# Twelve of 49 node tiles summed by fetched rows instead of eleven, fourteen fetches to nine steps, and their products in the bank of the transposes

## The reference

```python
h = jnp.maximum(_layernorm(x, axis=-1), 0.0)
x = x + _L0_gnn_ref(h, edge_index, edge_attr_64, W1, b1, W2, b2)   # mean of edge features, then a 2-layer MLP
h = jnp.maximum(_layernorm(x, axis=-1), 0.0)
x = x + _L1_gnn_ref(h, src, dst, w_neigh, w_self, b_self)

# _L1_gnn_ref(feat, ...):
summed = jax.ops.segment_sum(feat[src], dst, num_segments=n)
deg = jax.ops.segment_sum(jnp.ones_like(dst, dtype=feat.dtype), dst, num_segments=n)
h_neigh = (summed / jnp.maximum(deg, 1.0)[:, None]) @ w_neigh.T
rst = feat @ w_self.T + b_self + h_neigh
```

## Time and profile before

| | us |
|---|---|
| median of 3 runs | 1132.64 (1132.23 to 1134.74) |
| the profiled execution | 1135.44 |
| its span, first to last instruction | 1133.5 |
| first layer and edge lists | 0 to 455 |
| last preparation, PE nearly idle | 455 to 467.4 |
| loop over 38 dense tiles, with 11 near tiles between | 467.4 to 1130 |
| PE busy / DVE / ACT / POOL in the span | 1072.6 / 787.8 / 494.5 / 521.7 |
| mean granted clock | 0.985 |

### The profile page before, as it was taken

One profiled execution on the slowest core, in us unless ns is written; L12 is line 12 of the kernel. 1 busy time (PEld: TensorE's weight loads), 2 busy tenths in 40 slices (PEclk: granted clock), 3 DMA queues, 4 the chain that ended last, 5 costly groups with the idle time before them and its releaser, 6 DMA issues.

```text
span 1133.5 us, 29643 instructions
## 1 busy us (share of the span) xinstructions
PE 1072.6 (95%) x11380; PEld 792.0 (70%) x11380; DVE 787.8 (70%) x1849; ACT 494.5 (44%) x957; POOL 521.7 (46%) x502
## 2 busy tenths in 40 slices
PE   3689999999999999699999999999999999999998
PEld 2667777777777777467767777677677777776765
DVE  6778878887883667766766676766676767666762
ACT  4455646342212546444444444444444444444441
POOL 3011111110002664377576766774767676677520
PEclk9899999999999999699999999999999999999999
DMA  8776655555562221133233233332333333333210
GB/s 259 226 212 202 198 162 166 153 162 161 173 198 93 77 61 44 51 98 104 79 108 96 86 99 95 95 101 71 112 94 102 91 98 94 94 97 99 79 44 19
DMA packets 72618, 131.93 MB, mean 116 GB/s; under 512 B 12414, under 2 KB 32594, under 8 KB 72492
## 3 DMA queue, kind: packets, MB, share of 16 engines
q1 hardware_dynamic: 51820, 75.25, 21.7%
q0 software_dynamic: 20672, 55.00, 16.9%
HBM read 117.25 MB, written 12.95 MB: 115 GB/s over the span
## 4 chain that ended last, share of the span: by engine, by line
PE 87%; DVE 6%; DVEq 2%; ACT 2%; issue 2%; DMA 1%; ACTq 0%; SPq 0%
PE bank L1216 35%; PE couples L1209 10%; PE couples L1039 9%; PE bank L1235 7%; PE bank L984 7%; PE bank L996 6%; PE bank L978 2%; PE bank L1247 2%; PE bank L1227 2%; PE couples L1044 2%; PE couples L949 1%; DVE oreg L1647 1%; PE couples L984 1%; DVE oreg L1396 1%; DVEq L1511 1%
## 5 line engine op out<-in xcount | busy, mean ns | idle before, releaser
L1216 PE MATMUL bank<-hreg,areg 128*128 128x512 f16 x1862 | 457.0, 383 | 0.0
L629 POOL DMA_INDIRECT wide<-h_table,aggn x332 | 354.6, 1068 | 193.8 <-PE couples L1209 95.2
L847 ACT ACTIVATE areg<-couples 128x784 bf16<-128x784 f32 x304 | 250.3, 824 | 351.0 <-PE couples L1209 342.1
L1216 PEld LDWEIGHTS bank<-hreg,areg 128*128 128x128 bf16 x1862 | 240.4, 144 | 95.1 <-issue 1.6
L1647 DVE TENSOR_TENSOR hids<-iota,kreg 128x1024 bf16<-128x1024 f16 (+1 forms) x304 | 177.8, 626 | 110.0 <-PE couples L1209 108.9
L1647 DVE TENSOR_TENSOR oreg<-iota,kreg 128x1024 bf16<-128x1024 f16 (+1 forms) x304 | 177.7, 626 | 24.5 <-PE couples L1209 23.4
L1039 PEld LDWEIGHTS couples<-oreg,kreg 128*64 128x64 f32 x3232 | 117.2, 142 | 64.7 <-issue 63.6
L1039 PE MATMUL couples<-oreg,kreg 128*64 128x48 f32 x3232 | 138.5, 230 | 21.3 <-DVE oreg L1396 16.7
L597 POOL TENSOR_TENSOR xr<-xr,b2bc 128x512 f32 x25 | 33.9, 1356 | 221.0 <-ACT h0buf L719 221.0
L1396 DVE TENSOR_TENSOR oreg<-iota,wide 128x384 f32<-128x384 f32 x202 | 121.5, 602 | 4.4 <-issue 1.3
L996 PE MATMUL bank<-wide,hids 128*128 128x256 f32 x400 | 104.4, 398 | 0.0
(11 more groups left out here) (176 smaller groups left out, 1102.2 us busy)
## 6 DMA issues: line engine op xcount, KB each, us to landing
kreg<-in_edge_attr_dram SPq DMA_DIRECT2D x202, 256.0 KB, 2.8
h_table<-hreg SPq DMA_DIRECT2D x25, 256.0 KB, 2.2
xr<-in_x_dram SPq DMA_DIRECT2D x6, 1024.0 KB, 7.6
wide<-h_table,aggn POOLq DMA_INDIRECT x332
out_dram<-hbuf SPq DMA_DIRECT2D x38, 128.0 KB, 1.9
out_dram<-h0buf SPq DMA_DIRECT2D x10, 128.0 KB
wide<-in_L_gnn_W_dram SPq DMA_DIRECT2D x2, 512.0 KB, 8.5
hids<-h_table,aggn POOLq DMA_INDIRECT x64
```

What stands on the lines that cost most here:

```text
L629: pool.indirect_dma_start(near_rows(n % RING, w), None, table, bass.IndirectOffsetOnAxis(ap=nearsrc[:, k:k + 1], axis=0)).then_inc(s_rows[ ...
L847: act.activation(step.rearrange("p (a k) -> p a k", a=2), cpl[s % 2][:, :, 0:BC * KEYS], ACT.Copy).then_inc(s_adj, 1)
L1216: ins = pe.matmul(bank[4 + par], adj[:, par, :, h], htab[:, h, :], start=(h == 0), stop=(h == TN - 1))
```

## The change

One more node tile goes by index. GB is 7, TWICE 3, so DT = 37 dense tiles (296 steps) and GT = 12 near tiles (432 fetches). The pace of fetches is `k * 9 // 14`. The seven blocks of edge lists now cover tiles 36 to 49, four of which (36 to 39) also lie in the blocks of the dense tiles; the first 36 columns of keys and indices are skipped (UNUSED). A near tile's products go to bank 6, which held its transposes, and no longer to bank 7. So bank 7 is free for the next near tile after `sum_parts`, and `free` moves from step 2 of the tile after `finish` to step 5 of `finish`; the transposes that follow a near tile wait for its result (`s_res`) in place of the copy (`s_trs`).

```diff
-    GB = 6
-    TWICE = 2
+    GB = 7
+    TWICE = 3
...
+    NEAR0 = T - 2 * GB
+    UNUSED = (DT - NEAR0) * GC * WS
...
-    PACE = 7, 5
+    PACE = 14, 9
     fetch_step = [k * PACE[1] // PACE[0] for k in range(GT * GC * WS)]
...
-        free = (finish[-1] + 1) * ST + 2 if finish else 0
+        free = finish[-1] * ST + 5 if finish else 0
...
-                                            bass.IndirectOffsetOnAxis(ap=nearsrc[:, k:k + 1], axis=0)
+                                            bass.IndirectOffsetOnAxis(ap=nearsrc[:, UNUSED + k:UNUSED + k + 1], axis=0)
...
                 pe.wait_ge(s_sumN, m + 1)
                 pe.wait_ge(s_h1, m + 1)
-                if later(m):
+                if m > 0 and order[m - 1] >= DT:
+                    pe.wait_ge(s_res, m)
+                elif m > 0:
                     pe.wait_ge(s_trs, m)
...
                 if c == 0 and n > 0:
-                    pe.wait_ge(s_res, place[DT + n // GC - 1] + 1)
+                    pe.wait_ge(s_sumN, place[DT + n // GC - 1] + 1)
...
-                                products(place[DT + g], bank[7])
+                                products(place[DT + g], bank[6])
...
-                late = [spare[0:GR, b * SL:(b + 1) * SL] for b in range(GB - 2)] + [unreached[0:GR, 0:SL], layer1[0:GR, 0:SL]]
+                late = [spare[0:GR, b * SL:(b + 1) * SL] for b in range(GB - 3)] + [
+                    unreached[0:GR, 0:SL], layer1[0:GR, 0:SL], layer1[0:GR, SL:2 * SL]]
...
-                for t in range(DT, DT + TWICE):
+                for t in range(NEAR0, 2 * DB):
                     dve.scalar_tensor_tensor(noplace[:, NK:NK + 1], cntN[:, t:t + 1], NOKEY, noplace[:, NK:NK + 1], ALU.mult,
                                              ALU.add)
...
-                                result(DT + g, place[DT + g], 2, g or None, bank[7])
+                                result(DT + g, place[DT + g], 2, g or None, bank[6])
```

More of the change, by code:

```diff
@@ L130, in gnn_kernel @@
     assert TF % XL == 0 and XPARTS * SPAN == U - 1 and XL == 2 * SPAN and XPARTS == BODIES - 1 and FE == 64 and NP >= N + WIN
-    assert finish[-1] < DT - 1 and len(order) == TN and DT + 2 * GB == T and GT <= 2 * GB and GC % TOGETHER == 0 and 2 * TOGETHER <= RING and max(fetch_step) < STEPS - ST and T == TN + 1 and DB % KB == 0 and CB == U and BC * KEYS <= 512
+    assert finish[-1] < DT - 1 and len(order) == TN and NEAR0 <= DT and GT <= 2 * GB and GC % TOGETHER == 0 and 2 * TOGETHER <= RING and max(fetch_step) < STEPS - ST and T == TN + 1 and DB % KB == 0 and CB == U and BC * KEYS <= 512
     assert KEY0 == BESIDE + 1 and PAUSES[-1] == KB - 1 and E < 2 ** 24 and GR <= P and GB * GR <= 512
@@ L570, in _ @@
             pool.iota(gchunki[:, :], pattern=[[0, 1]], base=0, channel_multiplier=1)
-            pool.iota(gnode0[:, :], pattern=[[2 * P, GB]], base=P * DT, channel_multiplier=GW,
+            pool.iota(gnode0[:, :], pattern=[[2 * P, GB]], base=P * NEAR0, channel_multiplier=GW,
                       allow_small_or_imprecise_dtypes=True)
@@ L585, in _ @@
             pool.affine_select(out=tiles_near[:, :], in_=tiles_near[:, :], compare_op=ALU.is_ge, fill=1.0,
-                               base=-DT, pattern=[[-2, GB]], channel_multiplier=1)
+                               base=-NEAR0, pattern=[[-2, GB]], channel_multiplier=1)
             pool.affine_select(out=tiles_before[:, :], in_=tiles_before[:, :], compare_op=ALU.is_ge, fill=1.0,
@@ L1138, in _ @@
                 pe.matmul(bank[1][0:GR, 0:GB], below_windows[:, k, :],
-                          cntN[:, DT:DT + 2 * GB].rearrange("p (b k) -> p k b", k=2)[:, k, :], start=(k == 0), stop=False)
+                          cntN[:, NEAR0:T].rearrange("p (b k) -> p k b", k=2)[:, k, :], start=(k == 0), stop=False)
             pe.matmul(bank[1][0:GR, 0:GB], ones[0:T, 0:GR], totn[:, :], start=False, stop=True).then_inc(s_startp, 1)
@@ L1742, in one_near @@
                     dve.tensor_tensor(onenear[:, n % RING, :, :], iota16[:, 0:GW].unsqueeze(1).broadcast_to([P, WS, GW]),
-                                      nearkey[:, n * WS:(n + 1) * WS].unsqueeze(2).broadcast_to([P, WS, GW]),
+                                      nearkey[:, UNUSED + n * WS:UNUSED + (n + 1) * WS].unsqueeze(2).broadcast_to([P, WS, GW]),
                                       ALU.is_equal).then_inc(s_onenear, 1)
```

## The result

| set | before, median us (runs) | changed, median us (runs) | ratio | 95% interval |
|---|---|---|---|---|
| first | 1134.26 (12) | 1130.20 (12) | 0.9966 | 0.9952 to 0.9979 |
| second, another job | 1136.88 (12) | 1130.84 (7) | 0.9952 | 0.9934 to 0.9969 |
| third, another job | 1136.60 (12) | 1130.09 (7) | 0.9950 | 0.9931 to 0.9969 |

The forecast, 1125.6 against 1132.64 us, is a ratio of 0.9938. The first set excludes it, and it lies just inside the two others. The change is worth some 4.8 us (the mean of the three differences of means, weighted by their spread, with a standard error of 0.5), not 7.0. Executions of one and the same kernel differ by 3 to 7 us from lowest to highest, so a part of what follows is about where they differ.

The account below looks back on a forecast made before the run. The prediction took PE to bound the kernel (87% of the chain that ended last). Its terms, -13.6 + 2.6 + 0.8 + 2.2 + 1.0 = -7.0 us, took the median from 1132.64 to 1125.6 us, range 1121.8 to 1130.5.

Parts of the forecast that it names:

- The sum for the loop: Second layer's loop: -13.6 us dense tile gone, +2.6 near tile's bursts, +0.8 its wait for one-hots, +2.2 longer waits.
- The term of `one_near`: Loop, DVE: `one_near` ahead of one-hots PE already awaits delays them 0.20 us, eleven times: +2.2 us (0 to 3.1).
- The twelve waits: Loop: PE waits for DVE's one-hots twelve times, eleven of them near 0.82 us in place of 0.62.
- POOL's pauses beyond its 0.30 us: Loop: POOL keeps pace with 3% to spare; its waits for couples fall to some 20 us in all.
- The preparation: Before the loop: two more edge-list blocks to fetch, later `near_in`, longer `near_out` and more count additions, +1.0 us.
- The gap of `near_in`: Before the loop: `near_in` ends 1.7 us later; 1.05 us vanish in DVE's wait for ACT, the rest in its next waits.
- POOL at nothing: Loop: POOL's fetches, 1.37 us each against 1.417 available, cost nothing; rival that POOL becomes the bound, above 1130.4 us, 8%.
- the sign of being wrong: Loop: PE's bursts waiting for rows, a DMA named as releaser, more than 2 us in all, would show POOL was the bound.
- the lock of the two engines' ports: Loop: VectorE and GpSimd share SBUF ports exclusively; were each fetch to wait out a one-hot, POOL could not keep up.
- the hand-over of the bank: Loop, rival: transposes after a near tile wait for its result, up to 1 us per tile, 12 us, 1137 in all; 2%.
- a dearer preparation: Before the loop, rival: late edge lists pass through or the slow clock lasts a step longer, 1127 to 1129.5 us; 16%.
- from the stages to the median: Whole kernel: -7.0 us takes the profiled 1135.44 to 1128.4; the median, 2.8 us below at 1132.64, becomes 1125.6.

Follow-up runs that it names:

- thirteen: Against the changed kernel: a thirteenth tile by index, seven fetches to four steps, bursts and first near one-hots each a step later; 1149.81 us in one run.
- layout: Kernel before with the tile `wide` as long as the changed kernel makes it, work the same; 1.0005 of before (0.9992 to 1.0018).
- the two fronts: Kernel before and changed kernel, each with the second layer's loop left out, storing one tile of x; 473.3 and 472.5 us.
- both_late: Changed kernel with bursts a step later behind their fetches and `free` at step 6 of `finish`; 1124.90 us (0.9910 of before), again 1124.97 us (0.9907).
- landed4: Changed kernel with LANDED 4 in place of 3, so bursts and near one-hots stand one step later behind their fetches; 1131.04 us, 0.9953 of before.

## Why the prediction was right about the way and too high about the size

**The sum for the loop held.** It said 637.7 - 13.6 + 2.6 + 0.8 + 2.2 = 629.7 us from the third couples to the last. Measured were 629.9 and 630.0 in two profiles, 631.3 in the first, 629.3 without a wait for rows. (The prediction's 634.1 us end at 1107 and not, as it says, with the last couples, which start at 1110.64; its 292 steps are right for that stretch, and the sum does not suffer.) The term of `one_near`, 2.2 us, which the earlier trace rows priced at 0.20 us each, was measured alone at 2.17. The twelve waits, the dense products, copies and fetches came in the numbers named, and POOL's pauses beyond its 0.30 us came to 24.8 us (73.8 before), where some 20 were named.

**The preparation held.** 1.0 us was forecast, 0.6 to 0.8 came. The gap of `near_in` is swallowed, as was judged: PE and DVE wait for ACT there.

**POOL at nothing was a step that failed, in its reason more than its size.** The average was right: 1.37 us a fetch was taken, 1.358 measured in `thirteen`, where POOL hardly rests. But the lag was reckoned with an average spacing from the start on, and 3.4 us of it were called free. In the first tile each fetch meets a pair of one-hots, takes 1.36 us, and POOL runs at one a step; by chunk 5 it is 6 us late, and PE waits 0.4 to 1.8 us. The 1.8 us lie just under the sign of being wrong that the prediction set (more than 2 us). In the trace of before, the same 1.37 us fetches stood at 475 to 483 us; they were read as spread, not as a pattern with a place. The prediction weighed the lock of the two engines' ports as something that would hold up every fetch, and set it aside as only some were long; the last section shows that it holds up those that start inside a one-hot instruction. My two other rivals, the hand-over of the bank and a dearer preparation, did not come: no row of the changed kernel has PE waiting for `s_res` before its transposes.

**The step that failed in size was the last: from the stages to the median.** The sum was laid against one profiled execution and its distance carried over to the median, as if everything outside the loop stayed put. Of the 4.6 us between the forecast of 1125.6 and the median of 1130.20, 1.6 are the level: the median of before was 1132.64 in three executions and 1134.26 in twelve. The others are the size of the gain. The stages of the three profiles of the changed kernel, put together and set against the three of the kernel before (with `layout`), are 0.75 longer before the loop, 7.4 shorter in it (a mean of 630.4) and 0.5 longer in the tail, where one of three ran its last products at the lower clock: 6.1 us. The runs say 4.8, with a standard error of 0.5. The wait for rows and the tail, 0.7 and 0.5 us, are the part between 7.0 and 6.1 that the traces show, after 0.3 us won on the preparation.

**The rest, a little over 1 us, stays open.** It isn't the longer tile (`layout`, 1.0005). The spans of the same profiles differ by 4.5 us only, as the edge lists begin 1.6 us later in the three of the changed kernel (361.1 against 359.5); but they scatter from 358.0 to 363.6, so this may be chance, and the two fronts differ by 0.3 us with a standard error of 0.9. The mean granted clock, which is known for all executions but the first twelve of before, points to the clock outside the loop. Among executions of one kernel, 0.001 less of it goes with 0.5 us more (correlation -0.68 in 58 of before, -0.64 in 26 of the changed kernel). The 58 have a mean of 0.9849, the 26 of 0.9820, which would go with 1.5 us, the size of the rest. `both_late` has 0.9850, as before, and gains by means 10.1 and 10.9 us, where its stages give 9.9. But `landed4`, at 0.9840, gains 5.6 (standard error 0.8), where its stages give 7.7. Waits for rows in executions that no profile caught would explain why `both_late` lies so far below the changed kernel, but then `landed4`, which has none either, should lie below it too, and does not. So the clock is a likely cause and not a shown one, and why the changed kernel should be granted less no run shows.

## What to carry to other kernels

Price a stage from the stage's own starts and ends and expect it to hold to 0.1 us, but don't carry the result to a median through one profiled execution: take several of each kernel and compare stage by stage. Where a wait exists already, look what is queued between it and the instruction waited for: each 0.2 us there is paid in full, and moving it one step later costs nothing. An engine that keeps pace on average may still be late where its instructions fall into step with those of an engine that holds them up; lay the starts of the two side by side, and check the stretch where that happens, not the mean.

## What the runs showed of the hardware

A fetch by GpSimd that starts while a one-hot instruction runs on DVE is held until that instruction is nearly done. The pair of a step is an instruction of 0.69 us and one of 0.56, 1.17 together. Two cases, in the changed kernel's first profile:

```profile
478.14 1.17 DVE L1651 TENSOR_TENSOR hids<-iota,kreg 128x1024 bf16<-128x1024 f16 x2 [0.51 <-PE couples L1211]
478.28 1.37 POOL L631 DMA_INDIRECT wide<-h_table,aggn  x1 [0.30 <-PE couples L1211]
...
528.22 1.16 DVE L1651 TENSOR_TENSOR oreg<-iota,kreg 128x1024 bf16<-128x1024 f16 x2
528.95 1.25 POOL L631 DMA_INDIRECT wide<-h_table,aggn  x1 [0.30 <-issue]
```

The first fetch ends 1.51 us after the pair began. So do all 103 of the 432 fetches that start from 0.05 to 0.5 us into a first instruction, to within 0.02 us, whether they take 1.42 us (started at 0.09) or 1.06 (at 0.45). The second case starts in the second instruction of its pair; the 83 fetches that start 0.07 to 0.44 us into one end 1.37 to 1.39 us after it began. The 246 others take 0.96 us on average, 11 of them more than 1.05. With 0.95 us for a fetch alone, one that meets an instruction is held up to 0.13 us before that instruction's end in the trace: it loses what is left of it, not a fixed share. The other eleven traces of the loop give on average the same ends, 1.51 and 1.38 us, to 0.01 us. This also keeps the fetches of the first tile in step: whenever within the first instruction a fetch starts, it ends at 1.51, the next starts at 1.81, and that is 0.14 us into the next pair, since a step is 1.67.

The Trainium skill ("SBUF — State Buffer", SBUF: two separate sides) describes the lock on the ports that the two engines share: whoever starts first has it for the whole instruction, and a VectorE instruction with two SBUF inputs, as the one-hots are, takes it only against a GpSimd instruction that reads SBUF. The trace agrees with a wait to the end of the instruction: up to 0.47 us lost by a start 0.09 us into an instruction of 0.69 us. The section takes it, as an inference, that such a VectorE instruction leaves the writing of descriptors alone; these fetches are held all the same. They also read their indices (`aggn`) from SBUF; that this is why they are held is not shown.

The clock was the largest difference between executions of one kernel: 0.52 against 0.83 in the stretch of the first layer shown above, and eight last products in 3.3 or 2.0 us after the same two waits of 1.15 and 0.69 us.
